# Two cross-attention layers with an MLP on one core: value-difference mask, shared norm rows, a wider division and reordered first blocks

## The chip, the cores and the metric

The kernel runs on one core of a Trainium2 chip. The time is the device time of one launch in microseconds, the median of the runs shown. TensorE is called PE (its weight load PEld), VectorE DVE, ScalarE ACT, GpSimd POOL, and SyncE, which issues nearly all DMAs, SP.

## The reference

`x` holds 8 x 56 query rows of 256 numbers, `ctx` 8 x 1500 rows of 256. Two layers of cross-attention (H = 16 heads of K = 128) and an MLP of width 1024 follow each other:

```python
def _cross_attention(q_in, kv_in, wq, bq, wk, bk, wv, bv, wo, bo, bias_k, bias_v):
    qh = (q_in @ wq + bq).reshape(b, q_len, H, K)
    kh, vh = (kv_in @ wk + bk)..., (kv_in @ wv + bv)...
    kh, vh = concatenate([kh, bias_k]), concatenate([vh, bias_v])   # one extra key and value
    weights = softmax(einsum('bqhk,bthk->bhqt', qh, kh) / sqrt(K))
    return einsum('bhqt,bthk->bqhk', weights, vh).reshape(b, q_len, H * K) @ wo + bo
x = x + _cross_attention(layer_norm(x), ctx, ...)    # twice
x = x + gelu(layer_norm(x) @ w_fc1 + b_fc1) @ w_fc2 + b_fc2
```

## The kernel before

All products run as three fp32r products of a high and a low part. "hi" parts are rounded copies, mostly by ACT, "lo" parts the differences, by POOL for weights and context and by DVE for activations. Each engine works strictly in the order in which its block lists the work; semaphores join them.

A layer has three stages. **Query stage**: for each head, PE makes the queries (`queries`, 6 matmuls of 448 columns, line 748), ACT and DVE split them (`query_hi`, `query_lo`), PE carries them through the key weights (`carried_queries`, 6 matmuls, line 769), and ACT writes the result (line 1051, twice a head) to `qt`. The first two heads are done together in `first_queries` (line 714), term by term, as the norm's parts arrive. The four weight buffers `w_raw[u]`, `w[u]` are refilled head by head: SP loads `w_raw` (line 375) when POOL has made the old low part and DVE has made the head's key bias product (`key_bias_product`, lines 1271 and 1275), ACT makes the high part (`weight_hi`, line 1003), POOL the low part (`weight_lo`, line 534). In layer 0 the first batch's context comes in by quarters in the same SP and POOL queues (`load_nat`, `load_tr`, `nat_part_lo`, `tr_part_lo`), and the scores wait for the last quarter.

**Score and weight stage**: 8 batches, each with two groups of 4 and 3 tiles of 128 (head, query) rows and 12 chunks of 125 keys. PE works on the scores of chunk k (line 782) and the weighted context of chunk k - 17 (lines 799 to 801), which accumulates in one PSUM bank per tile, 256 columns of context, one of the sum (column D) and one of the extra key's weight (column D + 1). When a group ends, `normalized` turns the sum into `rden` (line 1406), takes the extra weight into `pn_extra` (line 1408), and ACT (even tiles, line 1076) and DVE (odd tiles, line 1410) write `on`; the banks are then free for the next group's line 799. Two chunks later DVE transposes `on` in `turn_context` (line 1418) for the moves by DMA.

**Output stage**: for each head PE projects the context to values (`head_context`, line 748 and one matmul for the extra key, line 823; `first_contexts` for the first two, line 837) and multiplies by the output weights (`output_rows`, 12 matmuls, line 843). The extra key's part is `p80`, the extra weights of all heads, and `dv80`, the difference of the value biases, both in 80 rows (high, low, high). POOL masks `p80` to one head at a time (`mask_extra`, line 666, 80 x 448) into two buffers `pm`. Then DVE takes the statistics of the rows (lines 1184 and 1189), POOL raises the variance to -1/2 (line 565), DVE forms `ln_r` (lines 1199 to 1203) and the normalized rows `xn` (line 1206, four instructions), PE transposes them (line 705) with idle matmuls around (`keep_busy`, line 698), and ACT and DVE make `ht` (lines 1009 to 1221). ACT copies the residual `xres` between (line 1157). The MLP uses the output stage's functions, with `gelu` in place of the split.

At the opening DVE takes the statistics of `x`, and between them the key bias difference `hdiff` (line 1296), which SP writes to DRAM (`dk_rows`, line 409) ahead of `vrow`, two weight loads, `mask`, `pick`, and the broadcast loads `dk_first` (line 386) and `dk_rest` (line 423) of what was written.

Of the kernel before, what the change touches and what calls it, by code (L numbers as in the profile page):

```python
# [34 lines left out]
RG = 4  # L35
# [44 lines left out]
LN_CHAIN = 4  # L80
# [7 lines left out]
def build(nc, x_rows, ctx_nat, ctx_tr, weights, cols, out_bias, head_rows, value_rows,  # L88
          ident_in, mask_in, pick_in, dk_rows, lb_flat, out):
    stack = ExitStack()  # L90
    with stack:
# [41 lines left out]
        ln_r = sb("ln_r", [RGP, RG], F32)  # L133
        p80 = sb("p80", [EXTRA, ROWS], F32R)
# [21 lines left out]
        on = sb("on", [P, GT[0], D], F32)  # L156
# [15 lines left out]
        pm = [sb(f"pm{s}", [EXTRA, ROWS], F32R) for s in range(2)]  # L172
# [59 lines left out]
        xn_ready, xt_mm = sem("xn_ready"), sem("xt_mm")  # L232
# [19 lines left out]
        pm_ready, oth_early, oth_hi, oth_lo = sem("pm_ready"), sem("oth_early"), sem("oth_hi"), sem("oth_lo")  # L252
# [7 lines left out]
        def settle(eng):  # L260
# [6 lines left out]
            "act": [saved, w_hi, h_hi, q_hi, qp_out, most_qs_hi, first_qs_hi, copied, exp_done, on_act, ot_out,  # L267
                    p80_hi, oth_early, oth_hi, c_hi, g32_ready],
            "dve": [filled, x_ready, ln_stats, ln_aggr, ln_chain, xn_ready, h32_ready, h_lo, dk_ready, cq_step, cq_ready,
# [3 lines left out]
            "pool": [zeroed, setup_step, nat_lo, tr_lo, w_lo, ln_pow, qs_hi, qs_lo, pt_lo, dv80_step, pm_ready],  # L273
# [255 lines left out]
        def _(pool):  # L529
# [54 lines left out]
            pool.wait_ge(xn_ready, INIT + RG)  # L584
# [6 lines left out]
            for l in range(LAYERS):  # L591
# [64 lines left out]
                for u in range(2):  # L656
                    weight_lo(l * JOBS + (H + u), u)
                pool.wait_ge(oth_lo, INIT + l * H + 2)
                weight_lo(l * JOBS + (H + 2), 2)

                def mask_extra(h, s, free):


                    pool.wait_ge(c_mm, INIT + free)
                    settle(pool)
                    nc.gpsimd.tensor_tensor(pm[s][:], as_f32(p80[:]), mask[:, ds(h, 1)].to_broadcast([EXTRA, ROWS]),  # L666
                                            ALU.mult).then_inc(pm_ready, 1)

                pool.wait_ge(consts_in, 16 * N_CONSTS)
                pool.wait_ge(p80_lo, INIT + l + 1)  # L670
                for s in range(2):
                    mask_extra(s, s, l * H)
                weight_lo(l * JOBS + (H + 3), 3)
                for u in range(2, 4):
                    mask_extra(u, u - 2, l * H + (u - 1))
# [7 lines left out]
                pool.wait_ge(xn_ready, INIT + (l + 1) * RG + RG)  # L683
# [8 lines left out]
        def _(pe):  # L692
# [7 lines left out]
            def norm_transposes(m):  # L700
                for g in range(RG):
                    pe.wait_ge(xn_ready, INIT + m * RG + g + 1)
# [7 lines left out]
            def first_queries(m, n, job):  # L710

                def term(u, a, part, c):

                    return mm(Q_BANK[u][:, 0:ROWS], w[u][:, a, c * P:(c + 1) * P], ht[:, part, c, :],
                              start=(a, part, c) == (HI, HI, 0), stop=(part, c) == (LO, DC - 1))
# [10 lines left out]
                for c in range(DC):  # L726
                    pe.wait_ge(h_lo, INIT + m * DC + c + 1)
                    for u in range(2):
                        last = term(u, HI, LO, c)
                        if c == DC - 1:  # L730
                            last.then_inc(q_mm, 1)
# [81 lines left out]
            def head_context(u, n, job, extra):  # L813
# [5 lines left out]
                if extra:  # L819
                    project(C_BANK[u][:, 0:ROWS], u, lambda m, c: oth[s][:, m, c, :],  # L820
                            ((oth_hi, INIT + n + 1, 0), (oth_lo, INIT + n + 1, 0)), True)
                    pe.wait_ge(pm_ready, INIT + n + 1)
                    mm(C_BANK[u][:, 0:ROWS], dv80[:], pm[s][:], start=False, stop=True).then_inc(c_mm, 1)  # L823
# [4 lines left out]
            def first_contexts(n, job):  # L828
# [58 lines left out]
            for l in range(LAYERS):  # L887
# [18 lines left out]
                first_queries(l, l * H, l * JOBS)  # L906
# [82 lines left out]
            for u in range(2):  # L989
                head_context(u, LAYERS * H + u, LAYERS * JOBS + u, False)  # L990
# [590 lines left out]
```

## Time and profile before

| what | us |
|---|---|
| median of 3 runs (1236.75 to 1239.4) | 1236.87 |
| the profiled execution's own time | 1234.94 |
| its span | 1233.1 |
| PE busy, share of the span | 1210.1, 98% |
| PEld, DVE, ACT, POOL busy | 1111.1, 833.2, 767.9, 894.0 |

A row of a timeline gives the start, the length of the piece, engine, line, operation, tiles, the count of instructions in it, and in brackets the idle time of the engine ahead of it with what ended that. A busy PE is not one at its peak, since the ends of its matmuls are modelled.

### The profile page before, as it was taken

The page shows a single profiled execution, that of the slowest core. Times are in us where ns is not written, and L with a number is a line of the kernel's source. Part 1 is how long each engine was busy: PE and PEld are TensorE (multiplying, and loading weights), DVE is VectorE, ACT ScalarE, POOL GpSimd, SP SyncE. Part 2 cuts the span into 40 slices and gives each one's busy share as a digit, 9 for nine tenths or more (in the row PEclk, how much of TensorE's full clock was granted, in tenths as well). Part 3 has the DMA queues.
Part 4 walks back from the last instruction along what each step waited for, and adds up shares of the span by engine and source line. Part 5 has one row for each costly group of instructions (what it writes and reads, how often), then busy time and mean ns, then how long its engine had stood idle before and what let it go on. Part 6 is the DMA issues. An engine that isn't in the chain of part 4 may idle for free. (4 is left out here: it accounts for less than half of the span.)

```text
span 1233.1 us, 26572 instructions
## 1 busy us (share of the span) xinstructions
PE 1210.1 (98%) x7736; PEld 1111.1 (90%) x7736; DVE 833.2 (68%) x1395; ACT 767.9 (62%) x1495; POOL 894.0 (72%) x744
## 2 busy tenths in 40 slices
PE   7999999999999999999999999999999999999998
PEld 6779999999999999998896999999999999999897
DVE  6765767676767676676755666676766666677654
ACT  5746666565666565676484656666666666667655
POOL 5737777777777787679551768686868686867882
PEclk9999999999999999999999999999999999999999
DMA  5401222222222222223320122222222222312231
GB/s 179 126 19 51 56 76 55 74 57 73 61 69 64 67 68 61 59 62 102 103 69 18 38 56 71 61 73 58 74 57 74 58 76 56 79 42 65 73 93 38
DMA packets 147720, 83.60 MB, mean 68 GB/s; under 512 B 121116, under 2 KB 122540, under 8 KB 147672
## 3 DMA queue, kind: packets, MB, share of 16 engines
q1 hardware_dynamic: 147128, 82.27, 25.5%
q10 hardware_dynamic: 544, 0.75, 0.2%
q8 instruction: 22, 0.36, 0.1%
q14 instruction: 26, 0.21, 0.1%
HBM read 68.56 MB, written 0.53 MB: 56 GB/s over the span
## 5 line engine op out<-in xcount | busy, mean ns | idle before, releaser
L607 POOL TENSOR_TENSOR pt<-slots,pt 125x512 fp32r<-125x512 f32 (+3 forms) x384 | 451.0, 1181 | 174.9 <-ACT slots L1069 167.6
L782 PE MATMUL psum<-qs,ctx 128*125 128x384 f32 (+1 forms) x2304 | 537.9, 370 | 3.0 <-ACT slots L1095 2.3
L782 PEld LDWEIGHTS psum<-qs,ctx 128*125 128x125 f32 x2304 | 394.2, 186 | 50.3 <-ACT slots L1095 10.1
L799 PE MATMUL psum<-ctx,pt 125*128 125x258 f32 (+1 forms) x1344 | 382.8, 285 | 1.4 <-ACT on L1076 0.5
L800 PE MATMUL psum<-ctx,pt 125*128 125x256 f32 (+1 forms) x1344 | 379.4, 282 | 0.0
L801 PE MATMUL psum<-ctx,pt 125*128 125x258 f32 (+1 forms) x1344 | 378.9, 282 | 0.0
L1068 ACT ACTIVATE pt<-slots 125x512 fp32r<-125x512 f32 (+3 forms) x384 | 221.3, 576 | 232.9 <-DVE slots L1356 221.9
L1368 DVE TENSOR_TENSOR t_max<-psum,t_max 125x512 f32<-125x512 f32 (+1 forms) x320 | 199.0, 622 | 200.9 <-PE psum L782 200.8
L1095 ACT ACTIVATE slots<-psum 125x512 f32<-125x512 f32 (+1 forms) x384 | 206.5, 538 | 121.7 <-DVE t_max L1368 112.6
L799 PEld LDWEIGHTS psum<-ctx,pt 125*128 125x128 f32 (+1 forms) x1344 | 253.5, 189 | 16.1 <-ACT on L1076 3.5
L800 PEld LDWEIGHTS psum<-ctx,pt 125*128 125x128 f32 (+1 forms) x1344 | 254.2, 189 | 6.7
L801 PEld LDWEIGHTS psum<-ctx,pt 125*128 125x128 f32 (+1 forms) x1344 | 254.8, 190 | 0.0
L1356 DVE TENSOR_TENSOR slots<-slots,psum 125x512 f32<-125x512 f32 (+3 forms) x384 | 231.6, 607 | 1.3
L1069 ACT ACTIVATE slots<-slots 125x512 f32<-125x512 f32 (+3 forms) x384 | 216.6, 564 | 0.0
L534 POOL TENSOR_TENSOR w<-w_raw,w 128x512 fp32r<-128x512 f32 x72 | 107.0, 1492 | 58.7 <-ACT w L1003 47.8
L543 POOL TENSOR_TENSOR ctx<-nat_stage,ctx 125x768 fp32r<-125x768 f32 (+1 forms) x60 | 103.5, 1725 | 26.1 <-DVE ctx L1235 26.1
L550 POOL TENSOR_TENSOR ctx<-tr_stage,ctx 128x750 fp32r<-128x750 f32 (+1 forms) x60 | 100.8, 1680 | 10.0 <-DVE ctx L1241 10.0
L558 POOL TENSOR_TENSOR qs<-qt,qs 128x384 fp32r<-128x384 f32 (+1 forms) x60 | 68.7, 1145 | 11.1 <-POOL qs L555 11.1
L843 PE MATMUL psum<-w,cs 128*112 128x256 f32 x480 | 63.6, 284 | 1.1 <-DVE cs L1485 1.1
L843 PEld LDWEIGHTS psum<-w,cs 128*112 128x112 f32 x480 | 61.4, 177 | 3.3 <-DVE cs L1485 1.7
L1241 DVE CAST ctx<-tr_stage 128x750 fp32r<-128x750 f32 (+1 forms) x60 | 62.5, 1041 | 0.9 <-DMA tr_stage<-ctx_tr 0.9
L1235 DVE CAST ctx<-nat_stage 125x768 fp32r<-125x768 f32 (+1 forms) x60 | 56.7, 945 | 7.1 <-DMA nat_stage<-ctx_nat 6.9
(105 smaller groups left out, 972.4 us busy)
## 6 DMA issues: line engine op xcount, KB each, us to landing
nat_stage<-ctx_nat SPq DMA_DIRECT2D x60, 375.0 KB
tr_stage<-ctx_tr SPq DMA_DIRECT2D x60, 375.0 KB, 3.1
w_raw<-weights SPq DMA_DIRECT2D x70, 256.0 KB, 2.7
qt<-turn SPq DMA_DIRECT2D x256, 32.0 KB, 2.0
qt<-turn SPq DMA_DIRECT2D x224, 24.0 KB, 1.9
dk_rest<-dk_rows SPq DMA_DIRECT2D x2, 768.0 KB, 5.7
w_raw<-weights ACTq DMA_DIRECT2D x2, 256.0 KB, 4.6
dk_first<-dk_rows SPq DMA_DIRECT2D x2, 256.0 KB, 4.7
```

What stands on the lines that cost most here:

```text
L534: nc.gpsimd.tensor_tensor(w[u][:, LO, :], w_raw[u][:], as_f32(w[u][:, HI, :]), ALU.subtract).then_inc(w_lo, 1)
L607: nc.gpsimd.tensor_tensor(split_weights(h, LO, c), logits(h, c), as_f32(split_weights(h, HI, c)), ALU.subtract).then_inc(pt_lo, 1)
L782: last = mm(scores(h, k), ctx_tr_chunk(half, a, c), qs[h][:, m, half, 0:R], start=(half, a, m) == terms[0], stop=(half, a, m) == terms[-1])
L799: mm(out_bank[:, 0:D + 2], hi, ctx_nat_hi(c), start=(c == 0), stop=False, skip_group_check=True)
L800: mm(out_bank[:, 0:D], hi, ctx_nat_lo(c), start=False, stop=False, skip_group_check=True)
L801: return mm(out_bank[:, 0:D + 2], lo, ctx_nat_hi(c), start=False, stop=(c == NCT - 1), skip_group_check=True)
L843: last = mm(Y_BANK[g][0:RGP, 0:D], cs[u][:, a, rows], w[u][:, m, D:2 * D], start=first and (a, m) == (HI, HI), stop=last_head and (a, m) = ...
L1068: go(split_weights(h, HI, c), logits(h, c), ACT.Exp)
L1069: go(logits(h, c), logits(h, c), ACT.Exp).then_inc(exp_done, 1)
L1095: go(slot(h, c), scores(h, k), ACT.Copy).then_inc(copied, 1)
L1356: V.tensor_tensor(logits(h, c), logits(h, c), shift(h, c), ALU.subtract).then_inc(sub_done, 1)
L1368: V.tensor_tensor(t_max[h][0:CT], scores(h, k), before, ALU.max).then_inc(max_done, 1)
```

## The change

Five edits come together.

1. **Mask on the value differences.** POOL multiplies `dv80` (80 x 128) by the head's mask into one of four buffers `dvm`; PE then uses `dvm[u]` as stationary and the whole `p80` as moving. The first four masks stand between POOL's two first weight splits. `first_contexts` does the extra key's matmul of a head right behind that head's projection.
2. **Norm rows on two engines.** DVE forms `ln_b` = -mean x `ln_r`, then rows 0 and 2 of `xn`; ACT forms rows 1 and 3 (`norm_rows`). The `xres` copies come after ACT's part of the norm.
3. **Division over the extra column.** `on` is D + 2 wide; ACT waits for `rden_ready` only; `pn_extra` is a copy of column D + 1 of `on` (`extra_weights`), made just ahead of the transpose.
4. **Opening and weights.** `hdiff` moves behind the statistics of all four row groups, to where DVE waits for POOL's power. The first two `query_lo` come ahead of the first four `key_bias_product`. `weight_hi` of head h + 3 comes in step h between `query_hi` and the two writes of `qt`, where `weight_hi` of head h + 4 stood behind those writes. At the end of layer 0 the fourth `key_bias_product` of the next layer moves behind the statistics, into the wait for the power.
5. **MLP.** Its first two blocks use the term-by-term order of `first_queries`, now `first_blocks`.

```diff
+        dvm = [sb(f"dvm{u}", [EXTRA, K], F32R) for u in range(4)]
-        pm = [sb(f"pm{s}", [EXTRA, ROWS], F32R) for s in range(2)]
...
+                def mask_values(h, u):
+                    nc.gpsimd.tensor_tensor(dvm[u][:], as_f32(dv80[:]), mask[:, ds(h, 1)].to_broadcast([EXTRA, K]),
+                                            ALU.mult).then_inc(dvm_ready, 1)
+                weight_lo(l * JOBS + H, 0)
+                for u in range(4):
+                    mask_values(u, u)
+                weight_lo(l * JOBS + (H + 1), 1)
+                pool.wait_ge(oth_lo, INIT + l * H + 2)
+                for u in range(2, 4):
                     weight_lo(l * JOBS + (H + u), u)
...
                         weight_lo(l * JOBS + quad * 4 + (H + 4 + u), u)
-                        mask_extra(quad * 4 + (u + 4), u % 2, l * H + quad * 4 + (u + 3))
+                        pool.wait_ge(c_mm, INIT + l * H + quad * 4 + (u + 1))
+                        mask_values(quad * 4 + (u + 4), u)
...
                     project(C_BANK[u][:, 0:ROWS], u, lambda m, c, u=u: oth[u][:, m, c, :], ...)
-                for u in range(2):
-                    pe.wait_ge(pm_ready, INIT + n + u + 1)
-                    mm(C_BANK[u][:, 0:ROWS], dv80[:], pm[u][:], start=False, stop=True).then_inc(c_mm, 1)
+                    pe.wait_ge(dvm_ready, INIT + n + u + 1)
+                    if u == 0:
+                        pe.wait_ge(p80_lo, INIT + n // H + 1)
+                    mm(C_BANK[u][:, 0:ROWS], dvm[u][:], p80[:], start=False, stop=True).then_inc(c_mm, 1)
...
-            for u in range(2):
-                head_context(u, LAYERS * H + u, LAYERS * JOBS + u, False)
+            pe.wait_ge(c_lo, INIT + LAYERS * H - 2)
+            first_blocks(LAYERS, LAYERS * JOBS, C_BANK, c_mm)
...
+            def norm_rows(m):
+                act.wait_ge(ln_chain, INIT + m * LN_CHAIN + LN_CHAIN)
+                for g in range(1, RG, 2):
+                    go(xn[:, g, :], Y_BANK[g][0:RGP, 0:D] if m else xres[:, g, :], ACT.Identity,
+                       bias=ln_b[:, g:g + 1], scale=ln_r[:, g:g + 1]).then_inc(xn_act, 1)
...
                             query_hi((u + 1) % 4, quad * 4 + (u + 1))
+                        if u == 0:
+                            weight_hi(l * JOBS + quad * 4 + 3, 3, l * 8 + quad)
+                        elif not last_quad:
+                            weight_hi(l * JOBS + quad * 4 + (u + 3), u - 1, l * 8 + quad + 1)
...
-                        if not last_quad:
-                            weight_hi(l * JOBS + quad * 4 + (u + 4), u, l * 8 + quad + 1)
...
-                    act.wait_ge(pn_ready, INIT + l * GROUPS + b * 2 + (h + 1))
+                    act.wait_ge(rden_ready, INIT + l * GROUPS + b * 2 + (h + 1))
-                        go(on[:, j], out_banks[j][:, 0:D], ACT.Copy,
+                        go(on[:, j], out_banks[j][:, 0:D + 2], ACT.Copy,
...
+                norm_rows(l + 1)
+                norm(l + 1)
+                act.wait_ge(xn_dve, INIT + (l + 2) * (RG // 2))
                 for g in range(RG):
-                    act.wait_ge(xn_ready, INIT + (l + 1) * RG + g + 1)
                     go(xres[:, g, :], Y_BANK[g][0:RGP, 0:D], ACT.Copy).then_inc(saved, 1)
-                norm(l + 1)
...
+                V.scalar_tensor_tensor(ln_b[:], ln_mv[:, :, 0], -1.0, ln_r[:], ALU.mult, ALU.mult).then_inc(ln_chain, 1)
-                for g in range(RG):
+                for g in range(0, RG, 2):
...
             def bias_differences():
+                dve.wait_ge(hrow_in, 16)
+                V.tensor_tensor(hdiff[:], hrow[:, 0], hrow[:, 1], ALU.subtract).then_inc(dk_ready, 1)
...
-                if g == 1:
-                    dve.wait_ge(hrow_in, 16)
-                    V.tensor_tensor(hdiff[:], hrow[:, 0], hrow[:, 1], ALU.subtract).then_inc(dk_ready, 1)
...
-                if l == 0:
-                    dve.wait_ge(dk_first_in, 16)
-                    for u in range(2):
-                        key_bias_product(l, u, u, 0, True)
                 query_lo(0, 0)
                 query_lo(1, 1)
                 if l == 0:
-                    for u in range(2, 4):
+                    dve.wait_ge(dk_first_in, 16)
+                    for u in range(4):
                         key_bias_product(l, u, u, 0, True)
...
-                    V.tensor_tensor(pn_extra[:, at], sums[:, D + 1], rden[:, at], ALU.mult).then_inc(pn_ready, 1)
...
+                def extra_weights(b, h):
                     dve.wait_ge(on_act, INIT + l * (2 * GROUPS) + b * 4 + (2 * h + 2))
                     dve.wait_ge(on_dve, INIT + l * (3 * B) + b * 3 + (2 + h))
+                    V.tensor_copy(pn_extra[:, tiles_of(batch_at(l, b), h)], on[:, 0:GT[h], D + 1]).then_inc(pn_ready, 1)
...
-                        if last_quad and l + 1 < LAYERS:
+                        if last_quad and l + 1 < LAYERS and u < 3:
...
-                norm(l + 1, lambda: None, lambda: None)
+                norm(l + 1, fourth_product if l + 1 < LAYERS else lambda: None)
```

## Rows read from the trace of the kernel before

**Rows 1.** Waits of PEld inside the score stage, layer 0, then layer 1: us, times, longest.
```profile
PEld psum L799 <- ACT on L1076: 2.5, 7, 0.4
...
PEld psum L799 <- issue: 3.3, 7, 0.5
```
**Rows 2.** Timeline, the end of one group in layer 0.
```profile
240.25 0.18 DVE L1406 RECIPROCAL rden<-psum 128x4 f32 x1 [0.77 <-PE psum L801]
240.56 0.16 DVE L1408 TENSOR_TENSOR pn_extra<-psum,rden 128x4 f32 x1
240.93 0.84 ACT L1076 ACTIVATE on<-psum,rden 128x256 f32<-128x256 f32 x2 [0.81 <-DVE pn_extra L1408]
```
**Rows 3.** Timeline, start of layer 0's output stage.
```profile
551.91 2.50 POOL L534 TENSOR_TENSOR w<-w_raw,w 128x512 fp32r<-128x512 f32 x2 [0.20 <-POOL dv L653]
...
554.44 2.66 PE L748 MATMUL psum<-oth,w 128*128 128x448 f32 x12
...
555.19 0.62 DVE L1490 TENSOR_TENSOR p<-psum,p 16x448 fp32r<-16x448 f32 x1 [0.40 <-ACT p L1122]
...
559.44 1.45 PEld L843 LDWEIGHTS psum<-w,cs 128*112 128x112 f32 x12 [0.83 <-DVE cs L1485]
```
**Rows 4.** POOL prices: lines 666 and 653 (ns min/median/max, first and last start), and a timeline row.
```profile
L666 POOL TENSOR_TENSOR pm<-p,mask x32: 922/930/1862, 556.5 to 1195.3; 80x448 fp32r<-80x448 f32 x32
...
L653 POOL TENSOR_TENSOR dv<-dv,dv x2: 963/965/967, 550.7 to 1146.8; 32x128 fp32r<-32x128 f32 x2
...
140.44 1.02 POOL L607 TENSOR_TENSOR pt<-slots,pt 125x384 fp32r<-125x384 f32 x1
```
**Rows 5.** Layer 1's output start: timeline; then busy PE, PEld, DVE, ACT, POOL, clock.
```profile
1150.54 2.66 PE L748 MATMUL psum<-oth,w 128*128 128x448 f32 x12
...
1155.24 2.12 PEld L843 LDWEIGHTS psum<-w,cs 128*112 128x112 f32 x12 [0.83 <-DVE cs L1485]
...
1153.00:1155.20 2.20, 1.15 (x4) 0.37 (x2) 0.68 (x1) 1.37 (x2) 2.20 (x3) 1.00 0.51 138
1155.20:1157.30 2.10, 2.06 (x12) 2.06 (x13) 1.96 (x2) 1.47 (x3) 2.10 (x3) 0.65 0.18 60
1157.30:1159.30 2.00, 2.00 (x7) 1.83 (x7) 1.68 (x2) 0.63 (x1) 1.45 (x2) 0.51 0.20 76
```
**Rows 6.** Timeline, opening and query stage of layer 0.
```profile
5.37 0.41 DVE L1296 TENSOR_TENSOR hdiff<-hrow 16x256 f32<-16x256 f32 x1 [0.26 <-DMA hrow<-head_rows]
...
15.51 0.42 DVE L1271 TENSOR_TENSOR g_prod<-w_raw,dk_first 128x256 f32<-128x256 f32 x1 [1.34 <-DMA dk_first<-dk_rows]
...
17.63 2.27 SPq L375 DMA_DIRECT2D w_raw<-weights  x2
...
23.25 0.63 ACT L1003 ACTIVATE w<-w_raw 128x512 fp32r<-128x512 f32 x1 [0.63 <-DMA w_raw<-weights]
...
44.21 0.63 ACT L1003 ACTIVATE w<-w_raw 128x512 fp32r<-128x512 f32 x1 [1.17 <-DMA w_raw<-weights]
...
58.84 4.01 PEld L782 LDWEIGHTS psum<-qs,ctx 128*125 128x125 f32 x18 [1.18 <-POOL ctx L550]
```
**Rows 7.** Timeline, the norm between the layers, with one row of the norm before the MLP.
```profile
605.33 0.40 DVE L1184 BATCH_NORM_STATS2 ln_stat<-psum 112x6 f32<-112x256 f32 x1
...
607.97 1.90 DVE L1206 TENSOR_SCALAR xn<-psum,ln_mv,ln_r 112x256 f32<-112x256 f32 x4
...
619.75 1.11 PEld L769 LDWEIGHTS psum<-qh,w 128*128 128x128 f32 x6 [0.57 <-ACT qt L1051]
...
1201.35 0.43 DVE L1184 BATCH_NORM_STATS2 ln_stat<-psum 112x6 f32<-112x256 f32 x1 [0.20 <-PE psum L843]
```
**Rows 8.** Query stage of layer 1: PE, PEld, DVE, ACT, POOL busy (instructions), clock.
```profile
621.00:645.30 24.30, 24.30 (x122) 22.52 (x121) 14.61 (x31) 22.08 (x41) 13.17 (x11) 1.00 0.32 86
```
**Rows 9.** Timeline, ACT at the MLP's start.
```profile
1207.86 1.28 ACT L1164 ACT_TABLE_LOAD   x1
1210.21 0.64 ACT L1164 ACTIVATE g<-psum,col 128x448 f32<-128x448 f32 x1 [1.08 <-PE psum L748]
```

More of the change, by code:

```diff
@@ L78 @@
 INIT = 4
-LN_CHAIN = 4
+LN_CHAIN = 5
 EXTRA = 80
@@ L133, in build @@
         ln_r = sb("ln_r", [RGP, RG], F32)
+        ln_b = sb("ln_b", [RGP, RG], F32)
         p80 = sb("p80", [EXTRA, ROWS], F32R)
@@ L655, in _ @@
                 pool.wait_ge(dv80_step, INIT + l * 2 + 2)
-                for u in range(2):
-                    weight_lo(l * JOBS + (H + u), u)
[L658 to L673, printed above, removed]
-                for u in range(2, 4):
-                    mask_extra(u, u - 2, l * H + (u - 1))
+                def mask_values(h, u):
+                    nc.gpsimd.tensor_tensor(dvm[u][:], as_f32(dv80[:]), mask[:, ds(h, 1)].to_broadcast([EXTRA, K]),
+                                            ALU.mult).then_inc(dvm_ready, 1)
+                pool.wait_ge(consts_in, 16 * N_CONSTS)
+                weight_lo(l * JOBS + H, 0)
[4 more added lines that the diff above has]
+                for u in range(2, 4):
+                    weight_lo(l * JOBS + (H + u), u)
                 with pool.Fori(0, QUADS - 1) as quad:
@@ L708, in norm_transposes, with first_blocks @@
                             last.then_inc(xt_mm, 1)
-            def first_queries(m, n, job):
+            def first_blocks(m, job, banks, done):
                 def term(u, a, part, c):
-                    return mm(Q_BANK[u][:, 0:ROWS], w[u][:, a, c * P:(c + 1) * P], ht[:, part, c, :],
+                    return mm(banks[u][:, 0:ROWS], w[u][:, a, c * P:(c + 1) * P], ht[:, part, c, :],
                               start=(a, part, c) == (HI, HI, 0), stop=(part, c) == (LO, DC - 1))
@@ L730, in first_queries @@
                         if c == DC - 1:
-                            last.then_inc(q_mm, 1)
+                            last.then_inc(done, 1)
             def residual(m):
@@ L834, in first_contexts @@
                             ((oth_hi, INIT + n + u + 1, 0), (oth_lo, INIT + n + u + 1, 0)), True)
-                for u in range(2):
-                    pe.wait_ge(pm_ready, INIT + n + u + 1)
-                    mm(C_BANK[u][:, 0:ROWS], dv80[:], pm[u][:], start=False, stop=True).then_inc(c_mm, 1)
+                    pe.wait_ge(dvm_ready, INIT + n + u + 1)
+                    if u == 0:
+                        pe.wait_ge(p80_lo, INIT + n // H + 1)
+                    mm(C_BANK[u][:, 0:ROWS], dvm[u][:], p80[:], start=False, stop=True).then_inc(c_mm, 1)
             def row_group(u, g, first, last_head):
@@ L1020, in _ @@
             go(act_ready[:], filler[:, 0:1], ACT.Copy)
-            for u in range(4):
+            for u in range(3):
                 act.wait_ge(w_in[u], 16)
@@ L1147, in output_quad @@
                             context_hi(quad * 4 + (u + 4), u % 2, l * H + quad * 4 + (u + 3))
-                        if not (first_quad and u == 0):
+                        if not (first_quad and u == 0) and not (last_quad and u == 3 and l + 1 < LAYERS):
                             weight_hi(l * JOBS + quad * 4 + (H + 4 + u), u, l * 8 + quad + 5)
@@ L1189, in aggregate, with norm @@
                 V.bn_aggr(ln_mv[:, g, :], ln_stat[:, g, :]).then_inc(ln_aggr, 1)
-            def norm(m, while_waiting, while_turning):
+            def norm(m, while_waiting):
                 base = m * LN_CHAIN
@@ L1293, in _ @@
                 statistics(0, g)
-                if g == 1:
-                    dve.wait_ge(hrow_in, 16)
-                    V.tensor_tensor(hdiff[:], hrow[:, 0], hrow[:, 1], ALU.subtract).then_inc(dk_ready, 1)
                 aggregate(0, g)
-            norm(0, bias_differences, value_difference)
+            norm(0, bias_differences)
+            value_difference()
             for l in range(LAYERS):
```

42 lines of the change are left out of this document (23 added, 19 removed).

## The prediction

> **What bounds the kernel now.** I read the page first, then the waits of PEld, then timelines of the places that the edits touch. PE is busy nearly throughout, so work taken from the other engines is worth nothing by itself; only places where PE waits count. The reader is to see three kinds. In the score stage PE waits once a batch, seven times a layer, when the second group's first tile needs a bank that ACT has still to empty: 0.36 us each in layer 0, 0.47 us in layer 1 [rows 1]. At the start of each output stage and each norm a chain over several engines leaves PE short of work [rows 3, 5, 7]. And the opening has a chain of its own: the scores of layer 0 begin when POOL delivers the last context quarter, not when PE has done its queries [rows 6].
>
> **Division.** ACT starts 0.21 us after line 1408 ends, and that line starts 0.13 us after the reciprocal's end. Freed from it ACT starts at 240.43 + 0.21 = 240.64 in place of 240.93, 0.29 us sooner [rows 2]. How much of PEld's gap is PE's loss? The matmul still running covers about 0.2 us of it (one of PE's 448-column matmuls takes 2.66 / 12 = 0.22 [rows 3]). So PE loses about 0.16 to 0.2 us a time in layer 0 and 0.3 in layer 1, less than or equal to the shift: 7 x 0.19 + 7 x 0.29 = 3.4 us. Two tail groups, one a layer, wait in the same way, some 0.15 us each: **-3.7 us**. Bounds: nothing, if the release is not what PE waits for, and -4.5. Two more columns are 2 in 256. The copy that replaces line 1408 (0.16 us [rows 2]) stands in front of a DVE transpose that only DMAs wait for, and behind it a chunk's maximum whose bank PE wants two chunks later; that covers it, and without cover it costs 16 x 2 x 0.16 = 5 us.
>
> **Mask on the differences.** In the steady part POOL's mask follows a weight split and ends before ACT delivers the next high part; shorter or longer by half, it stays there: 0. PE's matmul keeps its 448 columns: 0. At the stage's start it counts. Price of one mask of 128 elements: POOL's rows give 1.25 us for 512 elements [rows 3] and 1.02 for 384 [rows 4], 1.8 ns an element, so 1.02 - 256 x 0.0018 = 0.56; from the old mask, 0.92 at 448, it would be 0.92 - 320 x 0.0018 = 0.35. I take 0.5. The upper bounds are the rows for 128 elements, 0.965, and the old mask's slowest, 1.862 [rows 4].
>
> The GPSIMD Engine Reference of the Trainium skill (3.1, Elementwise) gives 4497 ns for a two-input operation on 2048 elements, 2.2 ns each where these rows give 1.8; a mask at that slope would be 0.46 and the sum 0.3 us lower. Its Key points add that POOL shares its SBUF interfaces with DVE operations that have two SBUF inputs; that speaks against masks laid beside DVE's splits, and is a rival below.
>
> Layer 0 then: first split ends 551.91 + 1.25 = 553.16, four masks to 555.16, second split to 556.41, PE's second projection from 556.56 for 1.33 us, extra matmul 0.2, `output_rows` at 558.1 in place of 559.44 [rows 3]. The other branch, ACT and DVE splitting the first head, starts from `p80` (low part done 555.81 [rows 3]), extra matmul to 556.3, 0.64 + 0.68 for the split with 0.15 of signals: 557.8, so the POOL branch ends last. **-1.3 us.** Layer 1 has the same offsets from PE's start (554.44 and 1150.54), so 1154.2 against 1155.24: **-1.0 us** [rows 5]. The later splits, ordered behind, are ready at 559.1 at worst, ahead of PE's next need.
>
> **The clock.** In layer 1 PE was busy 1.15 of 2.20 us before 1155.2, and the granted clock then was 0.65 and 0.51 over 4.1 us, half of 2.4 GHz; at full clock the same work takes 2.1 x 0.65 + 2.0 x 0.51 = 2.4 us, so the drop cost 1.7 us [rows 5]. With the stall shortened by 1 us and split in two I expect it to stay up: **-1.7 us**, bounds 0 and -1.7. TensorE: Matmul & The Clock Gate in the Trainium skill (Part 1) says that the clock is let through by recent activity; it would support a gain, but not say whether the remaining gap is short enough, so the sum does not rest on it.
>
> **Norms.** The statistics before layer 1 start their last group at 605.33. In the norm before the MLP, with no products ahead, the last group starts 0.20 us after PE's signal and PE's idle matmuls [rows 7]; the same in layer 0 would be at about 604.3. **-1.0 us**: the fourth product (about 0.9 us) moves into the wait for POOL's power of some 1.2 us. The `xn` rows come 0.475 us apart on DVE, 1.90 for four; on two engines, with `ln_b` of 0.16 and a signal in front, the last is ready after 1.2: **-0.7 us** [rows 7]. In layer 1's query stage `query_hi` of head 2 no longer stands behind `weight_hi`, so PE's 0.57 us wait at 619.75 goes; the split weights, now later in ACT's order, give back 0.15: **-0.4 us** [rows 7]. Bounds for the three, 0.5 to 2.3. The steady pitch is full PE work and stays: 122 matmuls in 24.30 us, all of it busy, so 2.4 us for the 12 of a head [rows 8]. ACT has 22.08 of the 24.30 to do, and by its new order a split weight arrives an estimated 0.6 us before PE wants it.
>
> **MLP.** The `xn` gain returns here, and PE's blocks end early, but ACT's copies of `xres` now stand between the norm and the table load: norm done at 1207.86 - 0.7 = 1207.2, four copies at the 0.42 of rows 2, load 1.28, `gelu` at 1210.1 against 1210.21 [rows 9]. **-0.1 us**, bounds +0.5 and -0.7.
>
> **Opening.** The statistics end sooner and the first queries start about 0.9 us sooner. But `hdiff` ends 1.1 us later (5.78 to about 6.86: two groups of statistics and `ln_v` now go first). SP waits for it at the head of its queue, and behind it stand `vrow`, the two weight loads, `mask`, `pick`, `dk_first`, `dk_rest`. DVE was idle 1.34 us until `dk_first` landed at 15.51; the weight load at 17.63 waits for the products behind it; ACT waited for that load until 23.25 [rows 6]. From there a chain repeats: load, high part, POOL's low part, POOL's context quarter, which frees the stage buffer for the next quarter and, behind it on SP, the next load. It returns after two rounds at 44.21, 10.5 us a round against 4 x 2.4 = 9.6 of PE [rows 8], and it ends in the context quarter that PE waits 1.18 us for at 58.84 [rows 6]. So PE's head start is lost and the shift stays: **+1.1 us**. Bounds: -0.9 if the chain takes up the shift, +1.6.
>
> **Sum.** -3.7 - 1.3 - 1.0 - 1.7 - 1.0 - 0.7 - 0.4 - 0.1 + 1.1 = -8.8 us. The profiled execution, 1234.94 us with a span of 1233.1, would become 1226.1 and 1224.3; its time lies 1.9 us under the median, so the median goes from 1236.87 to **1228.1**.
>
> **Rivals.**
> - *The clock drops all the same* in layer 1: 1229.8. For it: PE still has two short gaps. Against: layer 0 had as long a stall with no price in its next row (1.45 against 2.12 us for the same 12 loads [rows 3, 5]).
> - *Slow masks.* POOL lies between `output_rows` and both first heads. At 0.965 a mask, the second split ends 4 x 0.465 = 1.9 us later, both -1.3 and -1.0 turn to +0.6 and +0.9, and the clock stays low: 1228.1 + 3.8 + 1.7 = 1233.6. At the slowest old mask, 1.862, each layer loses 5.4 us against my sum: 1228.1 + 10.9 + 1.7 = 1240.7, **slower than before**. It decides from 1.5 us a mask on. For it: the 1.862 row; against: its median of 0.930 at 448 elements. This is the place where the skill's rule on shared SBUF interfaces would bite.
> - *The score stage's waits stay* (another release stands behind ACT's): 1231.8, and with masks of 0.965 as well 1237.3, no change.
> - *The opening gains* what its norm gains: 1226.1.
>
> **How the numbers follow.** Chances: the forecast 0.45, clock 0.15, masks at 0.965 0.12, score waits stay 0.09, these two together 0.05, opening gains 0.1, slow masks 0.04. The range from 1223.5 to 1234 takes in all but the last two slower cases. A difference under 0.2%, 2.5 us, can't be told from none; faster by more: 0.88, within: 0.08, slower: 0.04.
>
> **What would show it.** ACT's `on` 0.2 us behind the reciprocal and no PEld gap at the second groups; masks near 0.5 us; `output_rows` 3.7 us behind PE's first projection in both layers with the clock at 1.00; statistics of layer 0 right behind PE; the load now at 17.63 near 18.7 and the first scores near 59.9. I am wrong if the masks take a microsecond, if the gaps at line 799 remain, or if a PE wait appears in the query stages, where ACT's order changed for every head.

## The result, and the profile after

The changed kernel takes 1225.92 us (median of 4 runs, 1225.34 to 1226.65) against 1236.81 (1236.36 to 1239.4): a ratio of 0.9906, 95% interval 0.9893 to 0.9919, or 10.9 us less. Its profiled execution took 1225.35 us, 9.6 us under the 1234.94 of before, with a span of 1223.6. Cut at PE's first instruction of each stage, the two spans and those of two kernels with one part of the change each (below) are, in us:

| stage | before | changed | division alone | masks alone |
|---|---|---|---|---|
| opening and queries, layer 0 | 58.84 | 60.97 | 58.39 | 59.86 |
| scores, layer 0 | 495.60 | 493.77 | 493.42 | 496.03 |
| first contexts, layer 0 | 5.00 | 4.25 | 5.01 | 4.02 |
| rest of the output stage | 44.70 | 43.52 | 44.72 | 43.81 |
| norm between the layers | 7.17 | 5.58 | 7.15 | 7.04 |
| queries, layer 1 | 42.42 | 42.44 | 42.41 | 42.46 |
| scores, layer 1 | 496.81 | 494.09 | 494.35 | 496.76 |
| first contexts, layer 1 | 4.70 | 4.27 | 4.69 | 4.27 |
| rest of the output stage | 45.91 | 43.58 | 45.57 | 43.59 |
| norm and MLP | 31.99 | 31.09 | 31.93 | 31.83 |

The columns of the changed kernel less before: +2.13, -1.83, -0.75, -1.18, -1.59, +0.02, -2.72, -0.43, -2.33, -0.90, in sum -9.6. The norm before the MLP, up to PE's first block, is 0.63 of the last 0.90 (5.56 against 6.19), and the two first blocks are 0.25 (4.85 against 5.10).

Score stages. These are the waits of PEld in layer 1's, to be read against [rows 1] (waited for, us, times, longest):

```profile
PEld psum L798 <- issue: 1.3, 6, 0.2
...
PEld psum L798 <- ACT on L1086: 0.3, 1, 0.3
```

The seven waits of up to 0.5 us are down to six of 0.2; the one of 0.3 is the tail group's, 0.5 before. The group end of [rows 2] now reads, in the timeline:

```profile
241.84 0.18 DVE L1414 RECIPROCAL rden<-psum 128x4 f32 x1 [0.77 <-PE psum L800]
242.17 0.88 DVE L1417 TENSOR_SCALAR on<-psum,rden 128x258 f32<-128x258 f32 x2
242.24 0.84 ACT L1086 ACTIVATE on<-psum,rden 128x258 f32<-128x258 f32 x2 [0.52 <-DVE rden L1414]
```

ACT starts 0.40 us behind the reciprocal's start, 0.68 before.

First contexts of layer 0, against [rows 3] (timeline):

```profile
553.41 1.48 POOL L661 TENSOR_TENSOR dvm<-dv,mask 80x128 fp32r<-80x128 f32 x4
...
554.62 1.68 DVE L1487 TENSOR_TENSOR oth<-qt,oth 128x112 fp32r<-128x112 f32 x2 [0.41 <-ACT oth L1129]
...
554.74 1.46 PE L747 MATMUL psum<-oth,w 128*128 128x448 f32 x6
554.84 1.33 POOL L535 TENSOR_TENSOR w<-w_raw,w 128x512 fp32r<-128x512 f32 x1
...
556.33 0.62 DVE L1503 TENSOR_TENSOR p<-psum,p 16x448 fp32r<-16x448 f32 x1
...
557.10 0.44 PE L837 MATMUL psum<-p,dvm 80*128 80x448 f32 x1 [0.91 <-DVE p L1503]
```

A mask takes 0.37 us. But DVE's two small low parts (L1487) take 1.68 us beside POOL's weight split, where they took 0.46 before; so the low part of `p80` starts 1.59 us behind PE's first projection, 0.75 in [rows 3], and PE waits for it, not for POOL. `output_rows` starts 4.25 us behind PE's first projection, 5.00 before.

Layer 1, against [rows 5] (windows: start and end, length, then the busy time of PE, PEld, DVE, ACT and POOL with the counts of instructions, the granted clock, the DMA share, GB/s): the clock stays up.

```profile
1144.60:1149.00 4.40, 3.48 (x18) 2.60 (x17) 2.92 (x5) 2.12 (x5) 3.99 (x4) 1.00 0.42 122
1149.00:1153.00 4.00, 4.00 (x25) 3.82 (x26) 2.88 (x4) 3.02 (x5) 1.55 (x2) 1.00 0.46 127
```

The opening, against [rows 6] (timeline, then two windows as above):

```profile
6.50 0.41 DVE L1291 TENSOR_TENSOR hdiff<-hrow 16x256 f32<-16x256 f32 x1
...
16.42 1.05 DVE L1282 TENSOR_TENSOR g_prod<-w_raw,dk_first 128x256 f32<-128x256 f32 x1 [0.43 <-DMA dk_first<-dk_rows]
...
17.74 0.36 SPq L376 DMA_DIRECT2D w_raw<-weights  x1
...
25.16 0.63 ACT L1003 ACTIVATE w<-w_raw 128x512 fp32r<-128x512 f32 x1 [2.65 <-DMA w_raw<-weights]
...
26.25 1.10 PEld L768 LDWEIGHTS psum<-qh,w 128*128 128x128 f32 x6 [2.50 <-ACT qt L1063]
...
60.96 4.01 PEld L781 LDWEIGHTS psum<-qs,ctx 128*125 128x125 f32 x18 [1.24 <-POOL ctx L551]
```

```profile
25.00:27.00 2.00, 0.72 (x4) 0.72 (x5) 2.00 (x3) 1.84 (x4) 1.03 (x1) 1.00 0.48 180
27.00:31.50 4.50, 4.50 (x16) 3.98 (x15) 4.38 (x7) 2.85 (x7) 3.56 (x3) 0.62 0.28 77
```

`hdiff` starts 1.13 us later, the load of the fifth weight 1.6 us later, and ACT, whose weight split now stands ahead of the copies into `qt`, waits 2.65 us for a load while PE waits for those copies; the clock then falls. The end is the same as before: PE waits 1.24 us for the last context quarter, 2.1 us later.

Norms, against [rows 7] (timeline, layer 0 to 1):

```profile
602.71 0.43 DVE L1195 BATCH_NORM_STATS2 ln_stat<-psum 112x6 f32<-112x256 f32 x1 [0.20 <-PE psum L843]
...
605.47 0.99 DVE L1218 TENSOR_SCALAR xn<-psum,ln_mv,ln_r 112x256 f32<-112x256 f32 x2
605.59 1.02 ACT L1009 ACTIVATE xn<-psum,ln_b,ln_r 112x256 f32<-112x256 f32 x2 [2.19 <-DVE ln_b L1216]
```

and the MLP's start, against [rows 9]:

```profile
1198.42 1.19 ACT L1169 ACTIVATE xres<-psum 112x256 f32<-112x256 f32 x4
...
1199.62 1.28 ACT L1175 ACT_TABLE_LOAD   x1
...
1200.92 0.64 ACT L1175 ACTIVATE g<-psum,col 128x448 f32<-128x448 f32 x1
```

The query stage of layer 1, against [rows 7, 8]: no wait for `qt` at the third head, but a head's two pieces of six loads come at a pitch of 2.48 us, 2.43 before.

```profile
614.63 1.22 PEld L747 LDWEIGHTS psum<-ht,w 128*128 128x128 f32 x6
615.87 1.22 PEld L768 LDWEIGHTS psum<-qh,w 128*128 128x128 f32 x6
617.11 1.22 PEld L747 LDWEIGHTS psum<-ht,w 128*128 128x128 f32 x6
```

### The profile page after: what moved, and what is told of

Read it like the earlier page. It is cut to its first block, busy times and chain, and to the rows that moved or that the text cites. A ratio compares the mean times of both kernels' runs of the same rounds, so it can differ in the third digit from the quotient of the medians.

```text
span 1223.6 us, 26581 instructions
## 1 busy us (share of the span) xinstructions
PE 1202.5 (98%) x7736; PEld 1109.9 (91%) x7736; DVE 847.8 (69%) x1392; ACT 764.7 (62%) x1501; POOL 870.1 (71%) x744
## 4 chain that ended last, share of the span: by engine, by line
PE 93%; DVE 2%; DMA 2%; issue 1%; ACT 1%; POOL 1%; SPq 0%; DVEq 0%; POOLq 0%; ACTq 0%
PE psum L781 39%; PE psum L798 13%; PE psum L799 13%; PE psum L800 13%; PE psum L747 5%; PE psum L843 5%; PE psum L768 2%; DMA w_raw<-weights 1%; PE psum L697 1%; PE psum L822 0%; DMA dk_first<-dk_rows 0%; PE psum L793 0%; PE psum L788 0%; POOL ctx L551 0%; ACT slots L1079 0%
## 5 line engine op out<-in xcount | busy, mean ns | idle before, releaser
L781 PEld LDWEIGHTS psum<-qs,ctx 128*125 128x125 f32 x2304 | 394.4, 186 | 50.8 <-ACT slots L1105 10.1
L535 POOL TENSOR_TENSOR w<-w_raw,w 128x512 fp32r<-128x512 f32 x72 | 103.6, 1441 | 80.5 <-ACT w L1003 71.9
L1252 DVE CAST ctx<-tr_stage 128x750 fp32r<-128x750 f32 (+1 forms) x60 | 65.9, 1098 | 0.9 <-DMA tr_stage<-ctx_tr 0.9
```

Source lines behind the costliest of these rows:

```text
L535: nc.gpsimd.tensor_tensor(w[u][:, LO, :], w_raw[u][:], as_f32(w[u][:, HI, :]), ALU.subtract).then_inc(w_lo, 1)
L781: last = mm(scores(h, k), ctx_tr_chunk(half, a, c), qs[h][:, m, half, 0:R], start=(half, a, m) == terms[0], stop=(half, a, m) == terms[-1])
```

## The experiments

Three groups, each on one chip with its own runs of the kernel before; ratios are against those.

**Division alone**, in the kernel before.

```
-act.wait_ge(pn_ready, ...)          +act.wait_ge(rden_ready, ...)
-go(on[:, j], out_banks[j][:, 0:D]   +go(on[:, j], out_banks[j][:, 0:D + 2]
-V.tensor_tensor(pn_extra[:, at], sums[:, D + 1], rden[:, at], ALU.mult)
+V.tensor_copy(pn_extra[...], on[:, 0:GT[h], D + 1])   # in extra_weights, ahead of the transpose
```

> The kernel before with the division edit alone (ACT waits for the reciprocal, both divisions cover column D+1, the copy of the extra weights follows). Theory, from the changed kernel's trace: its score stages are 1.8 and 2.7 us shorter, and if the division alone does that, this kernel ends 4.5 us earlier, near 1232.3; by the terms of the prediction it would be 3.7 us, 1233.1. Rival one: the score stages got shorter through something else (where the batches' loads fall after the other edits), and this kernel stays at 1236.8. Rival two: POOL and DVE hold each other up at the new copy (it took 0.81 us beside a weight split at the stage's end), so that under 2 us are left, 1235.

1229.43 us, ratio 0.9948 (0.9934 to 0.9961), 6.3 us less. The table has the places: -2.18 and -2.46 in the score stages, 4.6 us together, nothing in the output stages' first contexts, and 0.45 in the opening, which scatters (below). Layer 1's 2.46 holds a pause of 0.67 us in one batch that the other profiles don't have. So the first theory holds for the stages, but 4.6 us lie just under the median's interval of 4.8 to 8.2. A part of what is left may be the clock, which no run separates: its five executions had granted clocks of 0.997 to 1.00 as a whole, the eleven of before on that chip 0.993 to 0.999. In layer 1 the clock happened to stay at 1.00, with the old masks, and this tells what the fall of [rows 5] had cost (windows and timeline):

```profile
1152.00:1154.00 2.00, 2.00 (x10) 1.53 (x9) 2.00 (x3) 1.27 (x3) 2.00 (x2) 1.00 0.26 98
1154.00:1156.00 2.00, 0.84 (x5) 0.75 (x5) 2.00 (x3) 0.72 (x1) 1.92 (x2) 1.00 0.22 65
```

```profile
1152.66 2.47 DVE L1484 TENSOR_TENSOR oth<-qt,oth 128x896 fp32r<-128x896 f32 x1
...
1155.19 0.68 PE L748 MATMUL psum<-oth,w 128*128 128x448 f32 x2 [1.16 <-DVE oth L1484]
```

PE at full clock runs into a wait of 1.16 us for the fourth head's low part, which DVE takes 2.47 us to make beside a weight split and a mask of POOL; in [rows 5]'s trace the same operation took 1.22. The rest of the stage is 45.57 us long in place of 45.91.

**Masks alone**, in the kernel before.

```
-pool: pm[s] = p80 * mask[:, h]      (80x448, two buffers, behind p80_lo)
-pe:   mm(C_BANK[u], dv80, pm[s])
+pool: dvm[u] = dv80 * mask[:, h]    (80x128, four buffers)
+pe:   mm(C_BANK[u], dvm[u], p80)
```

> The kernel before with the mask edit alone (mask times value differences, four buffers, PE's extra matmul with the masked weights). Theory A: besides the earlier first contexts (0.75 and 0.45 us) and the clock that stays up (1.7 us), the steady part of the output stages gains too, 1.2 and 0.6 us, because POOL was busy 35.3 of 38.0 us there and held PE up: together 4.7 us, 1232.1. Theory B, the prediction's: the steady part gains nothing, 1233.9. Theory C: neither the steady part nor the clock hangs on the masks, only 1.2 us remain, 1235.6.

1231.41 us, ratio 0.9963 (0.9949 to 0.9978), 4.35 us less. Theory A: first contexts -0.98 and -0.43, the rest of the output stages -0.89 and -2.32, in sum 4.6 us; the opening, which has none of the edit, came 1.0 us later in this profile. What changed in the steady part is seen in the low parts of `oth` (a line's instructions: ns min/median/max, first and last start). Before, then this kernel:

```profile
L1479 DVE TENSOR_TENSOR oth<-qt,oth x28: 1082/1222/1901, 559.5 to 1192.9; 128x896 fp32r<-128x896 f32 x28
```

```profile
L1476 DVE TENSOR_TENSOR oth<-qt,oth x28: 1080/1093/1093, 560.0 to 1189.8; 128x896 fp32r<-128x896 f32 x28
```

Every one of the 28 takes 1.08 or 1.09 us once the long masks are gone. That this is how PE gained in the steady part isn't shown: from 569 to 597 us POOL's busy time also went from 25.45 to 19.33 us, and the only waits of PEld listed there in before are two for "issue", 0.5 us together, none for DVE's low part.

**hdiff early**, in the changed kernel.

```
 statistics(0, g)
+if g == 1: dve.wait_ge(hrow_in, 16); V.tensor_tensor(hdiff[:], ...)
```

> The changed kernel with the subtraction hdiff back between the statistics of groups 1 and 2. Theory: the chain of the opening's loads starts 1.1 us earlier and hands that on to the first scores, 60.96 becomes 59.9, and the kernel ends 1 us earlier, 1224.9. Rival one: the load chain is held by ACT's new order of weight splits and not by hdiff, so nothing changes, 1225.9. Rival two: all of the 2.1 us that the opening lost come from it, 1223.8.

1225.22 us, ratio 0.9911 (0.9897 to 0.9925), five runs from 1223.42 to 1227.32: the median can't tell it from the changed kernel. The profiled one had first scores at 59.31 us, the load of the fifth weight at 16.77 and the clock at 1.00 throughout. It also had the query stage of layer 1 at a pitch of 2.43 us and 41.78 long, with the same code there: the 2.48 of the changed kernel's profile isn't the change's.

**Old weight order**, in the changed kernel: ACT's splits of the weights in the query stages as before.

```
-weight_hi(l * JOBS + quad * 4 + (u + 3), u - 1, ...)   # ahead of the copies into qt
+weight_hi(l * JOBS + quad * 4 + (u + 4), u, ...)       # behind them
```

> The changed kernel with ACT's old order of weight splits in the query stages (the split of the weight four heads ahead, behind the copies into qt; all four first weights split in the opening; the last quad of the output stage splits its fourth weight again). Theory: ACT no longer waits 1.55 and 2.65 us for loads ahead of copies into qt, so PE's wait of 2.5 us at 26.3 us goes and the first scores come 0.5 to 1 us earlier; layer 1 is even (its pitch per head 2.43 in place of 2.48 us gives 0.4 us, the wait of 0.57 for query_hi of head 2 returns): 1225.2. Rival one: PE's wait is covered by the context quarters that end the opening anyway, so the opening stays and the kernel is at 1225.9 or up to 0.4 us above. Rival two: without the new order the first scores come 2 us later, 1228.

1225.32 us, ratio 0.9909 (0.9895 to 0.9923). First scores at 60.76, as in the changed kernel (60.97 and 60.84): PE's wait at 26 us was covered, as rival one says. Layer 1's queries: pitch 2.43, the wait of 0.58 for the third head is back, 42.36 us. Against 41.76 (the second profile of the changed kernel, at the same pitch) the new order is worth 0.6 us there.

**Second split later**, in the changed kernel.

```
-weight_lo(l * JOBS + (H + 1), 1)
 pool.wait_ge(oth_lo, INIT + l * H + 2)
-for u in range(2, 4):
+for u in range(1, 4):
```

> The changed kernel with POOL's second weight split of each output stage moved behind the wait for DVE's low parts. Theory A (DVE and POOL hold each other up): DVE's two late low parts take 0.5 us in place of 1.7, the low part of p80 starts 1.1 us earlier, and the next limit is the moved split itself: output_rows about 3.7 us behind PE's first projection in place of 4.25, 0.5 us a layer, 1 us in all: 1224.9. Theory B (the split is what the second projection waits for, and DVE is slow for another reason): DVE's 1.7 us stay, the split comes later, and each layer loses 1 us: 1228.

1223.89 us, ratio 0.9891 (0.9876 to 0.9907). Theory A (timeline):

```profile
555.05 0.59 DVE L1486 TENSOR_TENSOR oth<-qt,oth 128x112 fp32r<-128x112 f32 x2 [0.41 <-ACT oth L1128]
...
555.84 3.78 POOL L535 TENSOR_TENSOR w<-w_raw,w 128x512 fp32r<-128x512 f32 x3 [0.52 <-DVE oth L1486]
555.95 0.62 DVE L1502 TENSOR_TENSOR p<-psum,p 16x448 fp32r<-16x448 f32 x1 [0.32 <-ACT p L1131]
```

DVE's low parts take 0.59 us again, and `output_rows` starts 3.55 and 3.54 us behind PE's first projection, 0.7 us sooner than in the changed kernel, in both layers; 0.35 and 0.12 are given back in the steady part (43.87 and 43.70), but four kernels with the changed output stages (changed again, hdiff early, old weight order, rows on DVE) lie there between 43.54 and 43.82 in layer 0, so the first is scatter for the most part.

**Idle matmuls in before**, a long and a short fill.

```
 for u in range(2):
+    fill(4)          # short: fill(2 + u)
     pe.wait_ge(pm_ready, ...); mm(C_BANK[u], dv80, pm[u])
+fill(5)              # short: fill(3)
```

> The kernel before with 13 idle matmuls in PE's waits of the first contexts (4 ahead of each masked matmul, 5 behind), so that the granted clock has no reason to fall there; the masks are the old ones. Theory A, from the run with the division alone, where the clock stayed at 1.00 and the output stage of layer 1 still took 45.57 us against 45.91: the drop cost only 0.3 us, since PE at full clock runs into the third head's low part, which DVE delivers late beside POOL's masks. This kernel gains 0.3 us against before. Theory B, the prediction's: the drop cost 1.7 us, and this kernel gains that.

> The kernel before with fewer idle matmuls in PE's waits of the first contexts (2 and 3 ahead of the two masked matmuls, 3 behind them: 0.4, 0.6 and 0.6 us by the 0.1 us that each half of one took in the last run, in waits of 0.49, 0.70 and 0.83), so that PE isn't held up and the clock should still stay. Theory A: from PE's first projection to its last output row the stage of layer 1 goes from 50.61 to 50.3 us, and the kernel gains 0.3. Theory B, the prediction's 1.7 us: 48.9, and 1.7 us.

Long: 1236.76 us, ratio 0.9999 (0.9989 to 1.0009). The fill held PE up (first contexts 5.75 and 5.78 us), so its median says little; the whole stage of layer 1 was 50.12 us. Short: 1235.98 us, ratio 0.9989 (0.9979 to 0.9999). First contexts and the rest in layer 1: 4.76 + 45.52 = 50.28 us against 50.61, theory A's 50.3. The median fell by 1.4 us, with an interval from 0.1 to 2.6 that holds both theories, so the theories are told apart by the stage alone. The clock there was 1.00, and the same wait stood in its place (windows, then waits of PEld in the output stage):

```profile
1155.00:1160.00 5.00, 5.00 (x37) 4.79 (x35) 1.72 (x4) 2.23 (x5) 4.38 (x5) 1.00 0.56 160
1160.00:1165.00 5.00, 4.02 (x25) 3.42 (x24) 4.85 (x5) 3.64 (x6) 5.00 (x5) 1.00 0.20 53
```

```profile
PEld psum L753 <- DVE oth L1486: 1.4, 1, 1.4
```

What holds for layer 1 doesn't hold for layer 0. There the low part comes in time at full clock, and one profile of a kernel with the old masks (hdiff late in before, below) shows what the same drop costs in that place (window):

```profile
564.20:567.60 3.40, 3.40 (x14) 3.33 (x15) 2.83 (x3) 1.83 (x4) 3.40 (x3) 0.50 0.26 82
```

The rest of layer 0's output stage took 46.03 us, against 44.66 to 44.73 in the four other profiles with the old masks (44.70 in before's): 1.33 us. In layer 1 of the same profile the clock fell too, and the rest took 45.89 us, as in before.

**Old mask price**, in the changed kernel: one more POOL operation a head, which nobody reads.

```
 mask_values(quad * 4 + (u + 4), u)
+nc.gpsimd.tensor_tensor(spare[:], p80[:, 0:424], mask[:, h], ALU.mult)
```

> The changed kernel with one more POOL operation per head in the steady part of the output stages: a product of p80 (80x424, close to the old mask's 80x448) and the mask into a spare tile that nobody reads or waits for, behind the new mask. Theory A (what the output stages gained beyond their first contexts comes from POOL's shorter work beside DVE's low parts): POOL's operation takes 1 to 2.7 us and DVE's low parts go from 1.09 to 1.2 to 1.9 us, and each output stage gets 1 to 2 us longer: 1227.9 to 1229.9. Theory B (that gain came from the masks being ready before the first low part of p80, and the steady part has slack on both engines): no change, 1225.9.

1236.05 us, ratio 0.9991 (0.9982 to 1.0): the output stages' rest took 51.69 and 47.06 us, 8.2 and 3.5 more. Up to the last heads both layers lost 3.4 to 3.5; layer 0 lost the rest at its end, where the clock was 0.51 from 607.8 to 611.3. The direction is theory A's, but POOL is now the bound itself (busy 28.00 of 28.00 us from 569 to 597, with a split, a mask and 0.89 us more for each head), so the run doesn't show that the old masks cost PE time by way of DVE and not by way of POOL. The lines of the mask and of DVE's low parts:

```profile
L664 POOL TENSOR_TENSOR dvm<-dv,mask x32: 392/822/1259, 554.4 to 1198.4; 80x128 fp32r<-80x128 f32 x32
```

```profile
L1499 DVE TENSOR_TENSOR oth<-qt,oth x28: 1074/2793/3043, 560.1 to 1196.6; 128x896 fp32r<-128x896 f32 x28
```

The same two operations take 0.39 and 1.09 us in the changed kernel.

**Rows on DVE**, in the changed kernel: all four `xn` rows on DVE.

```
+V.tensor_scalar(xn[:, g + 1, :], rows_of(m, g + 1), ...)   # behind the one of g
-go(xn[:, g, :], ..., ACT.Identity, bias=ln_b, scale=ln_r)  # ACT's norm_rows
```

> The changed kernel with all four xn rows on DVE again (ln_b still computed). Theory, the prediction's term: each of the two later norms gets 0.7 to 0.9 us longer (four rows 0.475 us apart against two and two in 1.0), the opening too, but its gain is lost in the load chain: 1.6 us in all, 1227.5. Rival: the norm before the MLP doesn't feel it, since ACT's xres copies and the table load end last there: 0.9 us, 1226.8.

1226.9 us, ratio 0.9916 (0.9902 to 0.993). By its profile the norm between the layers is 6.35 us against 5.58, norm and MLP 31.75 against 31.09: 0.77 and 0.66, in sum 1.43, between the two forecasts.

**The changed kernel again, both mends, and hdiff late in before.**

> The changed kernel as it is, a second time, as the yardstick of this group. Theory: 1225.9, first scores between 60.7 and 62.0 us. In its first profile the query stages ran at 2.48 us a head and in three of the other runs with the same code there at 2.43: if the 2.48 belongs to this build, it shows again and the query stage of layer 1 takes 42.4 us; if it changes from execution to execution, it may be 2.43, and the stage takes 41.8.

> The changed kernel with hdiff back between the statistics and POOL's second weight split of each output stage behind DVE's low parts. Theory: the gains of the two add, 1.5 to 2 us from the opening and 1.4 from the first contexts (output_rows 3.55 us behind PE's first projection), and the kernel is at 1222.5 against 1225.9. Rival: the opening's 1.7 us were the scatter of one profile (the old opening alone gave first scores at 58.4 to 60.3 us in four profiles), and only the 1.4 us stay: 1224.5.

> The kernel before with the subtraction hdiff moved behind the norm's first step, as in the changed kernel, and nothing else. Theory: the load of the differences, and with it the chain of the weight loads, starts 1.1 us later, and the first scores come 1 to 2 us later than the 58.4 to 60.3 us of the other profiles with the old opening; the kernel is 1 to 2 us slower than before. Rival: the chain takes the shift up, no change, and the 2 us that the changed kernel's opening lost come from its other edits there.

The changed kernel again: 1225.22 us, ratio 0.9903 (0.9888 to 0.9917); first scores at 60.84, pitch 2.43, query stage 41.76. Both mends: 1224.73, 0.9896 (0.9883 to 0.991); the 0.7 us in each layer's first contexts are there (3.42 and 3.54), but first scores came at 61.44, and the median isn't better than with the second split alone (0.9891). That one is the fastest kernel measured, some 1 to 2 us under the changed one, with intervals that overlap. hdiff late in before: 1237.89, 1.001 (1.0 to 1.002), first scores at 63.53; the interval holds no change as well as 1 to 2 us, so neither theory nor rival is ruled out. The profiles of all kernels give the opening's scatter ("clock falls": when the granted clock went from 1.00 to 0.50; in two of them it stayed there for 6.8 us):

| opening | clock falls, before 32 us | fifth weight's load | first scores |
|---|---|---|---|
| old: before, division alone | no fall | 16.19, 15.90 | 58.84, 58.39 |
| old: masks alone | 10.6 | 17.08 | 59.86 |
| old: long fill | 9.5, 19.7 | 17.80 | 60.32 |
| old: short fill | 18.8, for 6.8 us | 17.82 | 63.60 |
| changed (twice), second split later, old mask price | 25.9 to 27.6 | 17.74 to 17.88 | 60.84 to 61.95 |
| changed, old weight order | 9.8, 23.5 | 17.90 | 60.76 |
| changed, rows on DVE | 28.2 | 18.45 | 61.87 |
| changed, hdiff early | no fall | 16.77 | 59.31 |
| changed, both mends | 10.1, 27.1 | 17.82 | 61.44 |
| old, hdiff late | 18.1, for 6.8 us | 18.24 | 63.53 |

The same opening lies up to 5 us apart from one kernel to another. In most of the late ones the clock fell only behind the load, so it can't be what made the load late; but from the load to the first scores it takes 42.5 to 42.8 us where the clock doesn't fall behind the load, 42.5 to 44.2 where it does, and 45.8 and 45.3 in the two with 6.8 us at 0.50. In the kernel with both mends the fall came first: the clock was 0.76 and 0.82 from 8 to 16 us, its first product came 1.04 us later than with hdiff early alone (17.14 against 16.10), and the load by the same 1.05. There the two `query_lo`, which the changed order puts ahead of the products, ended at 17.23 and 16.18: with hdiff early the products wait for PE's first queries, and no longer for `dk_first`, which landed at 15.73 and 15.61.

## Why the prediction was right or wrong

The forecast was 1228.1 us, the range 1223.5 to 1234.0; it came out at 1225.92, faster, as forecast. By the steps:

- **Division, -3.7: right mechanism, size too small.** Alone it took 2.18 and 2.46 us from the score stages. For the second groups the term was right: from a batch's first reciprocal to its second, the run is 0.21 us shorter in layer 0 and 0.29 in layer 1, against 0.19 and 0.29 taken. What was missing is the other half of each batch, priced at nothing: from the second reciprocal to the next batch's first it is 0.13 and 0.20 shorter. In the trace of before, PEld waits there for the same ACT division, 0.08 and 0.15 us, too short to stand in the list of waits.
- **Masks at the stage's start, -1.3 and -1.0: right direction, branch wrong.** "The POOL branch ends last" failed. The masks were cheaper than the 0.5 us taken (0.37), and the other branch became the later: DVE's low parts, 0.46 us in the trace of before, took 1.7 beside the weight split that the new order puts there. Measured -0.75 and -0.43, and the run with the second split moved shows the contention: DVE's time is back at 0.59, and the first contexts are 0.7 a layer shorter.
- **"shorter or longer by half, it stays there: 0": wrong.** With the masks alone the rest of the output stages gained 0.89 us in layer 0 and 2.32 in layer 1. The prediction asked when POOL's mask ends, and not what it does to the DVE operations beside it, which took up to 1.9 us in place of 1.09. It kept the Trainium skill's rule on shared interfaces for a rival, with the opposite sign. How the 0.9 us came about in the steady heads stays open: through DVE, or through POOL itself, which was busy for 25.45 of 28.00 us.
- **Clock, -1.7: the sum was near by luck, the step wrong.** In [rows 5] the low clock covered a wait that PE would have had anyway. With the old masks and full clock, by chance in one run and by short fills in another, the stage got 0.35 and 0.33 us shorter. Some 1.4 of layer 1's 2.3 us come from the wait for the fourth head's low part, which is gone (from the first `output_rows` to the next 5.77 us with the division alone, 4.36 with the masks alone); the rest is spread over the heads behind, as in layer 0. The 1.7 worked out from busy time at a lower clock is near the price where PE has no wait behind the drop: in layer 0, in the one profile that has it there, the drop cost 1.33.
- **Norms, -1.0 and -0.7: right** (-1.59 together; 0.77 of it are the rows, by the run that undoes them, and the rest goes with the statistics, now 0.20 us behind PE, which no run undoes). **`query_hi`, -0.4:** 0 in the first profile and -0.66 in the second: the gain is there (0.6 against the old order), and a pitch of 2.48 in place of 2.43 us hid it in the first.
- **MLP, -0.1: mis-sized**, -0.90. ACT's four copies of `xres` took 1.19 us in place of the 1.7 taken, and the table load's end stayed just where PE's first block ends, so that the norm's shorter chain came through: 0.66 by the run that undoes the rows. The other 0.25 lies in the two first blocks, whose new order no run tests by itself.
- **Opening, +1.1: right sign, size open.** +2.1 in the profile compared, but old openings lie between 58.4 and 63.6. That hdiff alone makes it is not shown: its delay in the kernel before moved the median by +0.1%, with an interval of 0 to +0.2%, which holds the forecast's 1.1 us too. The chain that the prediction followed is there. It lacked two things: the products now stand behind `query_lo`, so that even with hdiff early they started at 16.10 us, against 15.51 in before; and the clock, which falls in some executions and not in others, at several places of the chain.

The forecast lay 2.2 us above the result. Only 0.8 of it lies in the sum (-8.8 against -9.6 between the profiles), and that nearness is part luck: the terms for the clock and the steady masks, -1.7 and 0, stand against about -0.3 and -3.2, the masks' start was taken 1.1 us too large, and the division, the MLP and the opening missed by 0.9, 0.8 and 1.0, not all the same way. The rest is where the profiles lie: before's 1.9 us under its median, the changed one's 0.6. By the medians division and masks alone give 6.3 + 4.35 = 10.7 us of the 10.9, by the stages 4.6 + 4.6 = 9.2 of 9.6; the norms' gains and the opening's loss about cancel.

## What to carry to other kernels

Before you price a stall by the clock at which the work behind it ran, look for the next wait: at full speed PE may only reach it sooner. Here the same drop cost 0.3 us in one layer and 1.3 in the other. A wait that a list leaves out as too short still counts when it comes back in every batch. And when POOL and DVE work on SBUF at the same time, price both together: moving or shrinking an operation on one changes the time of the other, also where neither seems to be the bound. A gain found in one profile of a stage that loads from memory needs a second profile before it is believed.

## What the runs showed of the hardware

- POOL and DVE slow each other. A DVE operation on two SBUF operands of 896 elements takes 1.09 us alone, up to 1.9 beside POOL's 448-element masks, up to 2.47 beside a weight split and a mask, and a median of 2.79 in the run with the extra POOL operation; two of 112 elements take 0.46 to 0.59 or 1.68 together; POOL's 128-element mask 0.39 or a median of 0.82. DVE's operations on PSUM (`cs`, 0.67 to 0.68 us) didn't change beside the same POOL work. The GPSIMD Engine Reference of the Trainium skill (Key points) says that POOL shares its SBUF interfaces with DVE's operations on two SBUF inputs; the traces agree, and here the loss is sometimes POOL's (two masks in 3.60 us in the kernel before) and sometimes DVE's.
- A head of the query stage takes 2.43 us in some profiles and 2.48 in others, from the first steady head to the last, in kernels with the old code there (2.48 with the long fill) and with the new (both values for the changed kernel itself). The granted clock was 1.00 in both. What sets it stays open; over 13 heads it is 0.65 us.
